# Low parts of expert weights: accumulating DMAs in place of subtractions

## The chip, the cores and the metric

The kernel runs on one core of one Trainium2 chip, as one program with an instruction stream for each engine, written out by hand with semaphores between them. The metric is the device time of one execution in microseconds, the median of several runs. Below, "span" is the time from the first to the last instruction in the one execution that was profiled.

## The reference, cut to what matters

The input is x (4 x 256 tokens of 256 values). First a gated state-space layer (a convolution, a recurrence over 256 positions with 16 states per channel, an output scaled by silu of the normalised x) is added to x. Then follows a layer of eight experts, of which each token uses two:

```
logits = x @ gate_w                       # 1024 x 8
top_logits, top_idx = top_k(logits, 2);  top_w = softmax(top_logits)
for e in range(8):
    h = silu(x @ w0[e]) * (x @ w1[e])     # w0, w1: 8 x 256 x 512
    out += cw[:, e] * (h @ wo[e])         # wo: 8 x 512 x 256
```

All is float32.

## The kernel before, in words

**Split products.** The expert products run on operands in a rounded float32 format (`fp32r`). To keep the precision each operand is split into a rounded part ("hi") and what is left ("lo"), and a product is the sum of three terms: x_hi w_hi + x_hi w_lo + x_lo w_hi (`product`, L1048). So w0 and w1, 4 MB each, need a hi and a lo copy in SBUF. Each is cut into 16 parts of 128 x 512 (expert e, half k), 32 in all, in the order of `SPLITS`: w1 of experts 0 to 5, w0 of all, w1 of experts 6 and 7. The last sit on space that other tiles occupy until the end of the scan. ScalarE rounds a part (`upper`, L529), and after that one of three engines subtracts: GpSimd 22 parts (`lower`, L405), VectorE six (`lower`, L1343), TensorE four (`low_part`, L994 and L995: the part times the identity plus the rounded part times its negative, moved out by ScalarE at L688).

**Scan.** From about 36 to 149 us the recurrence runs in 64 steps n over 128 x 512 tiles. In a step VectorE computes the drive (L1243) and the scan (L1249), ScalarE the decay as an exponential (L619) and every second step a copy of the C rows (L615), GpSimd the product of state and C (`times_C`, L414), TensorE the sum over states in PSUM (L853) and the spread of B and C rows (L832, L839). Four state buffers go round (`RING`), so VectorE's drive of step n waits for GpSimd's product of step n - 4. The tuples `SPLIT_AT` and `UPPER_AT` give the steps in which ScalarE rounds a part; GpSimd subtracts that of `SPLIT_AT` after its product of the same step. Other tuples put softplus steps, normalisations and logits of the first half of the tokens into the scan.

**Routing.** After the scan the second half is gated, normalised and routed; VectorE works out the tiles of tokens (23 `SLOTS` of 128 rows, each for one expert), TensorE makes the tables by one-hot matmuls (L1020, L1025). SyncE's queue is in order: the store of the first half (`store_x2`), WO loads of 0.5 MB each (L335) as their space comes free, two stores of normalised rows `x_rows` to DRAM (L325) and another store. GpSimd waits for both `x_rows` stores and the table, and gathers rows of a tile by an indirect DMA (L438). TensorE fills pauses with matmuls whose result nobody reads (`WARM`, `keep_busy`, L1013 and L1032), turns the tile (L1039), ScalarE rounds it (`xT_out`, L699), VectorE subtracts (`split_x`, L1472), and the first `gate` starts.

**Expert loop.** For each of the 23 tiles TensorE does gate, up (six matmuls each, L1048), the turn of the hidden tile (L1070) and down (twelve, L1084). x tiles are turned and rounded one tile ahead. The results are added to the output by an indirect accumulating DMA of 128 rows (L452).

Of the kernel before, what the change touches and what calls it, by code (L numbers as in the profile page):

```python
# [66 lines left out]
def build(nc, x, ctx_1024, g_xattn, g_ffn, in_proj_w, conv_w, conv_b, x_proj_w, dt_proj_w, dt_proj_b,  # L67
          A_log, D, gate_w, w0, w1, wo, out):
    stack = ExitStack()
    with stack:  # L70
# [12 lines left out]
        at_W0_hi = nc.sbuf_base  # L83
# [22 lines left out]
        at_W1_hi = nc.sbuf_base  # L106
# [132 lines left out]
        SPLIT = [bank[i] for i in (4, 0, 1, 7)]  # L239
# [28 lines left out]
        W_hi_ok, W_lo_pool, W_lo_dve, xT_split = map(sem, ("W_hi_ok", "W_lo_pool", "W_lo_dve", "xT_split"))  # L268
        W_lo_ps, W_lo_act, last_hc, mask_sum, count_ps = map(sem, ("W_lo_ps", "W_lo_act", "last_hc", "mask_sum", "count_ps"))
# [23 lines left out]
        def hi_part(i):  # L293
            w, e, k = SPLITS[i]
            return (W0_hi, W1_hi)[w][:, e, k, :]

        def lo_part(i):
            w, e, k = SPLITS[i]
            return (W0_lo, W1_lo)[w][:, e, k, :]
# [56 lines left out]
        def _(pool):  # L356
# [46 lines left out]
            def lower(i):  # L403
                pool.wait_ge(W_hi_ok, i + 1)
                pool.tensor_tensor(lo_part(i), whole_part(i), hi_part(i), ALU.subtract).then_inc(W_lo_pool, 1)  # L405

            def times_C(at, end):
                for n in range(at, end):
# [6 lines left out]
                    if n in SPLIT_AT:  # L415
                        lower(SPLIT_AT.index(n))
# [40 lines left out]
        def _(act):  # L457
# [128 lines left out]
            def decay(at, end):  # L586

                for n in range(at, end):
# [12 lines left out]
                    if n in SPLIT_AT:  # L601
                        if n == SPLIT_AT[0]:
                            act.wait_ge(ld["w1"], 16 * E)
                        if SPLITS[SPLIT_AT.index(n)] == (0, 0, 0):
                            act.wait_ge(ld["w0"], 16 * E)
                            act.wait_ge(delta_copied, 2)
                            act.wait_ge(one_plus, 2 * NQ)
                        upper(SPLIT_AT.index(n))
                    if n in UPPER_AT:
                        upper(EARLY + UPPER_AT.index(n))  # L610
# [147 lines left out]
        def _(pe):  # L758
# [263 lines left out]
            low_part(3)  # L1022
# [514 lines left out]
```

## Time and profile before

| | |
|---|---|
| runs, us | 300.47, 300.55, 301.75; median 300.55 |
| span of the profiled execution, us | 296.1, so its median run has 4.45 us around the span |
| busy: PE, DVE, ACT, POOL | 261.7, 226.3, 188.1, 180.1 us |
| share of the chain that ended last: PE, DVE, POOL, ACT | 57%, 15%, 6%, 4% |
| DMA: bytes and share of 16 engines, SyncE's queue / GpSimd's | 16.41 MB, 15.8% / 6.03 MB, 12.7% |
| mean granted TensorE clock | 0.980 of full speed |

PE is TensorE (PEld its weight loads), DVE VectorE, ACT ScalarE, POOL GpSimd, SP SyncE; a "q" behind a name is the engine's sequencer. The busy shares are means over three stages with different limits, so they don't say what a change in one stage is worth. A name of a tile that lies on another's space (WO for delta and zs, for instance) is that of the first tile there.

### The profile page before, as it was taken

What the parts mean: (1) busy time and instruction counts of PE and PEld (TensorE: products, weight loads), DVE (VectorE), ACT (ScalarE), POOL (GpSimd) and SP (SyncE); (2) the same over time, 40 slices, a digit from 0 to 9 for tenths busy, and PEclk for the clock granted to TensorE, in tenths of its full rate; (3) what the DMA queues carried; (4) which work ended last, traced back from release to release, by engine and by line L of the source; (5) the groups of instructions that cost most, each with busy time, mean ns of one, the idle gap of its engine ahead of it and who ended that gap; (6) DMA issues with size and microseconds to landing.
All of it is one profiled execution on the core that took longest, in us unless ns stands there. A gap on an engine that the chain in (4) does not pass through costs nothing.

```text
span 296.1 us, 4704 instructions
## 1 busy us (share of the span) xinstructions
PE 261.7 (88%) x1170; PEld 174.6 (59%) x1171; DVE 226.3 (76%) x396; ACT 188.1 (64%) x349; POOL 180.1 (61%) x162
## 2 busy tenths in 40 slices
PE   7984696899888998888889999999999999999970
PEld 6432242334345354433366658989898989898850
DVE  2939999999999998999978967656665656565630
ACT  3894587866775657778679636575757575756540
POOL 5100469898999898999880241546464656555242
PEclk9996899999999999999999999999999999999996
DMA  7699400000000001000069520333232323333322
GB/s 235 199 395 388 158 1 0 2 1 0 0 0 3 1 0 71 0 0 2 1 213 371 199 71 19 46 63 51 57 52 54 53 53 53 53 56 50 39 22 31
DMA packets 16659, 22.70 MB, mean 77 GB/s; under 512 B 2554, under 2 KB 10274, under 8 KB 16642
## 3 DMA queue, kind: packets, MB, share of 16 engines
q1 hardware_dynamic: 11456, 16.41, 15.8%
q0 software_dynamic: 4416, 6.03, 12.7%
q10 hardware_dynamic: 770, 0.06, 0.2%
q8 instruction: 7, 0.11, 0.2%
q14 instruction: 10, 0.08, 0.1%
HBM read 17.38 MB, written 5.11 MB: 76 GB/s over the span
## 4 chain that ended last, share of the span: by engine, by line
PE 57%; DVE 15%; issue 13%; POOL 6%; ACT 4%; DMA 1%; POOLq 1%; DVEq 0%; SPq 0%; ACTq 0%
PE PZ L1084 11%; PE PD L1048 11%; PE PU L1048 11%; PE PY L853 6%; DVE states L1243 6%; POOL hC L414 5%; PE PY L1070 4%; DVE states L1249 3%; DVE u L1169 2%; PE PZ L1039 2%; DMA early<-in_L_xattn_in_proj_w 1%; PE PZ L905 1%; PE PU L839 1%; PE PU L832 1%; PE PZ L894 1%
## 5 line engine op out<-in xcount | busy, mean ns | idle before, releaser
L414 POOL TENSOR_TENSOR hC<-states,WO 128x512 f32<-128x512 f32 x63 | 79.6, 1277 | 14.5 <-PE PY L853 9.3
L1249 DVE TENSOR_TENSOR_SCAN states<-PD,states 128x512 f32<-128x512 f32 x64 | 77.6, 1214 | 1.1 <-ACT PD L619 0.9
L853 PE MATMUL PY<-hC,ident 128*128 128x512 f32 x128 | 67.1, 607 | 4.1 <-POOL hC L414 3.9
L452 POOL DMA_INDIRECT out<-lg,y_at x23 | 36.9, 1605 | 49.5 <-ACT lg L727 41.8
L619 ACT ACTIVATE PD<-WO,Aneg 128x510 f32<-128x510 f32 x64 | 43.9, 689 | 19.2 <-DVE states L1249 16.5
L1243 DVE TENSOR_TENSOR states<-PU,WO 128x512 f32<-128x512 f32 x64 | 42.8, 671 | 0.5 <-POOL hC L414 0.4
L438 POOL DMA_INDIRECT hC<-x_rows,x_at x23 | 27.2, 1183 | 23.5 <-DMA x_rows<-u 13.6
L711 ACT ACTIVATE hidT_hi<-PY 128x512 fp32r<-128x512 f32 x23 | 13.8, 598 | 37.8 <-PE PY L1070 35.7
L1478 DVE TENSOR_TENSOR dA<-PU,dA 128x512 f32<-128x512 f32 x23 | 15.9, 692 | 28.5 <-PE PU L1048 28.5
L1490 DVE TENSOR_TENSOR WO_lo<-WO,WO_hi 128x512 fp32r<-128x512 f32 x46 | 29.8, 689 | 9.4 <-issue 9.3
L853 PEld LDWEIGHTS PY<-hC,ident 128*128 128x128 f32 x128 | 22.3, 189 | 15.5 <-POOL hC L414 11.1
L720 ACT ACTIVATE WO_hi<-WO 128x512 fp32r x46 | 26.5, 624 | 3.0 <-issue 0.6
L405 POOL TENSOR_TENSOR W_lo<-W,W_hi 128x512 fp32r<-128x512 f32 x22 | 28.4, 1296 | 0.0
L832 PE MATMUL PU<-BC,sel 128*128 128x512 f32 x32 | 16.9, 528 | 11.5 <-ACT WO L615 5.6
L615 ACT ACTIVATE WO<-PU 128x512 f32<-128x512 f32 x32 | 19.0, 593 | 12.3 <-PE PU L839 12.2
L832 PEld LDWEIGHTS PU<-BC,sel 128*128 128x128 f32 x32 | 6.2, 194 | 32.7 <-issue 31.8
L839 PE MATMUL PU<-BC,sel 128*128 128x512 f32 x32 | 17.7, 552 | 6.2 <-DVE states L1243 6.1
L1482 DVE TENSOR_TENSOR hidT_lo<-PY,hidT_hi 128x512 fp32r<-128x512 f32 x23 | 15.9, 692 | 5.1 <-ACT hidT_hi L711 4.9
L529 ACT ACTIVATE W_hi<-W 128x512 fp32r<-128x512 f32 x32 | 19.3, 618 | 0.0
L839 PEld LDWEIGHTS PU<-BC,sel 128*128 128x128 f32 x32 | 6.1, 191 | 21.5 <-issue 21.4
L1048 PE MATMUL PD<-W_hi,xT_hi 128*128 x46 | 16.4, 437 | 0.0
L705 ACT ACTIVATE dA<-PD 128x512 f32<-128x512 f32 x23 | 13.7, 597 | 4.1 <-PE PD L1048 4.1
(251 smaller groups left out, 501.2 us busy)
## 6 DMA issues: line engine op xcount, KB each, us to landing
W<-in_L_ffn_w SPq DMA_DIRECT2D x16, 512.0 KB, 10.6
WO<-in_L_ffn_wo SPq DMA_DIRECT2D x8, 512.0 KB, 6.9
xs<-in_x SPq DMA_DIRECT2D x2, 512.0 KB, 5.4
out<-xs SPq DMA_DIRECT2D x2, 512.0 KB, 3.4
x_rows<-u SPq DMA_DIRECT2D x2, 512.0 KB, 4.6
early<-in_ctx SPq DMA_DIRECT2D x1, 512.0 KB, 4.1
hC<-x_rows,x_at POOLq DMA_INDIRECT x23
out<-lg,y_at POOLq DMA_INDIRECT x23, 3.8
```

Of the source, the lines that this page charges most:

```text
L405: pool.tensor_tensor(lo_part(i), whole_part(i), hi_part(i), ALU.subtract).then_inc(W_lo_pool, 1)
L414: pool.tensor_tensor(hC[:, n % 2, :], states[:, n % RING, :], C_rep[:, pair % C_RING, :], ALU.mult).then_inc(hc_done, 1)
L438: pool.indirect_dma_start(out=x_tile[s % 2], out_offset=None, in_=x_rows, in_offset=bass.IndirectOffsetOnAxis(ap=x_at[:, s:s + 1], axis=0) ...
L452: pool.indirect_dma_start(out=out, out_offset=bass.IndirectOffsetOnAxis(ap=y_at[:, s:s + 1], axis=0), in_=y_tile[s % 2], in_offset=None, c ...
L619: act.activation(DEC[n % 2].rearrange("p (b l) -> p b l", b=QB)[:, :, 1:L], delta[2 * q + h].rearrange("p (b l) -> p b l", b=QB)[:, :, 1:L ...
L839: pe.matmul(BCR[(pair + 1) % 2], sel[:, DS + pair % DS:DS + pair % DS + 1].to_broadcast((P, P)), BC[:, pair // DS, :], start=True, stop=Tr ...
L853: pe.matmul(PY[:, h, :], ident[:, :], hC[:, n % 2, :], start=False, stop=(m == DS - 1)).then_inc(y_done, 1)
L1048: mm = pe.matmul(dest[i][:, :], x[i][:, k, :], w[:, bass.ds(expert, 1), k, :].rearrange("p o m -> p (o m)"), start=(n == 0), stop=(n == le ...
L1084: mm = pe.matmul(bank[7][:, i * DX:(i + 1) * DX], x[:, k, :], w[:, k, :], start=(n == 0 and k == 0), stop=(n == 2 and k == 3))
L1243: dve.tensor_tensor(states[:, n % RING, :], BCR[pair % 2], du[2 * q + h], ALU.mult).then_inc(dbu_done, 1)
L1249: dve.tensor_tensor_scan(states[:, n % RING, :], DEC[n % 2], states[:, n % RING, :], 0.0, ALU.mult, ALU.add).then_inc(scan_done, 1)
L1490: dve.tensor_tensor(WO_lo[i][:, cut, :].rearrange("p k n -> p (k n)"), WO[:, bass.ds(expert, 1), cut, :].rearrange("p o k n -> p (o k n)") ...
```

## The change

ScalarE no longer writes a rounded part beside the weight, but its negative over the weight itself. Groups of four parts (two experts, 1 MB) are then copied by SyncE inside SBUF to the place of the lo parts, and GpSimd issues a DMA that adds the weights once more from DRAM onto that copy: w - round(w). All 32 parts take this way, so the three kinds of subtraction go. Seven groups are issued from GpSimd inside the scan at `LOWER_AT`, the eighth after it; the eighth copy waits until the scan's tiles on its space are done with, ahead of the WO loads in SyncE's order. As only negated rounded weights are left, x tiles get a negated rounded copy as well (`xT_neg`, one more ScalarE instruction per tile), and the terms become x_neg w_neg + x_hi w_lo + x_neglo w_neg. All roundings lie in the scan. Matmuls that fill pauses are counted by `SPINS`.

```
-WARM = 1
-SPLIT_AT = (3, 6, 9, 12, 15, 18, 24, 26, 31, 33, 36, 39, 41, 44, 47, 49, 52, 54)
-UPPER_AT = (50, 53, 56, 57, 59, 60, 62)
+UPPER_AT = (3, 4, 6, 9, 11, 12, 15, 18, 20, 21, 23, 26, 28, 29, 31, 33, 34, 36, 38, 39, 41, 43, 46, 47, 49, 50, 52, 53, 55, 56, 58, 61)
+LOWER_AT = (15, 24, 32, 41, 50, 56, 62)
+SPINS = (4, 1, 2)
...
+        W0_neg, W1_neg = overlay("W0_neg", [P, E, 2, MH], at_W), overlay("W1_neg", [P, E, 2, MH], at_W + E * 2 * MH * 4)
+        W0_lo, W1_lo = overlay("W0_lo", [P, E, 2, MH], at_W0_lo), overlay("W1_lo", [P, E, 2, MH], at_W1_lo)
...
 # SyncE
+            def copy_neg(g):
+                w, e, _ = SPLITS[4 * g]
+                sp.wait_ge(W_neg_ok, 4 * (g + 1))
+                sp.dma_start((W0_lo, W1_lo)[w][:, e:e + 2, :, :].bitcast(F32), (W0_neg, W1_neg)[w][:, e:e + 2, :, :].bitcast(F32)).then_inc(W_copied[g], 16)
+            for g in range(3):
+                copy_neg(g)
+            sp.wait_ge(delta_copied, 2)
+            sp.wait_ge(one_plus, 2 * NQ)
+            for g in range(3, 5):
+                copy_neg(g)
             store_x2(0)
+            for g in range(5, 7):
+                copy_neg(g)
             sp.wait_ge(hc_done, NT - 1)
             sp.wait_ge(exp_done, NT)
             sp.wait_ge(dbu_done, NT)
+            sp.wait_ge(c_ps, NT // 2)
+            sp.wait_ge(b_ps, NT // 2)
+            sp.wait_ge(base_ps, NQ)
+            copy_neg(7)
             load_WO(0)
...
 # GpSimd
-            def lower(i):
-                pool.wait_ge(W_hi_ok, i + 1)
-                pool.tensor_tensor(lo_part(i), whole_part(i), hi_part(i), ALU.subtract).then_inc(W_lo_pool, 1)
+            def lower(g):
+                w, e, _ = SPLITS[4 * g]
+                pool.wait_ge(W_copied[g], 16)
+                pool.dma_start((W0_lo, W1_lo)[w][:, e:e + 2, :, :], (w0, w1)[w][e:e + 2].rearrange("e (k p) m -> p e k m", p=P),
+                               accum_op=ALU.add).then_inc(W_lo_in[w], 16)
...
-                    if n in SPLIT_AT:
-                        lower(SPLIT_AT.index(n))
+                    if n in LOWER_AT:
+                        lower(LOWER_AT.index(n))
...
-            for i in POOL_SPLITS:
-                lower(i)
+            for g in range(len(LOWER_AT), len(SPLITS) // 4):
+                lower(g)
...
 # ScalarE
-                act.activation(hi_part(i), whole_part(i), ACT.Copy).then_inc(W_hi_ok, 1)
+                act.activation(neg_part(i), whole_part(i), ACT.Copy, scale=-1.0).then_inc(W_neg_ok, 1)
...
-            act.wait_ge(b_ps, NT // 2)
-            act.wait_ge(c_ps, NT // 2)
             normed(range(QBLK))
-            for i in range(EARLY + len(UPPER_AT), EARLY + 9):
-                upper(i)
             x2_out(2)
             x2_out(3)
-            for i in range(EARLY + 9, len(SPLITS)):
-                upper(i)
             root(1)
...
-            for j in range(len(PE_SPLITS)):
-                act.wait_ge(W_lo_ps, j + 1)
-                act.activation(lo_part(PE_SPLITS[j]), SPLIT[j], ACT.Copy).then_inc(W_lo_act, 1)
...
                 act.activation(xT_hi[i].rearrange("p k t -> p (k t)"), bank[6][:, i * DX:(i + 1) * DX], ACT.Copy).then_inc(xT_ok, 1)
+                act.wait_ge(xT_ok, s + 1)
+                act.activation(xT_neg[i].rearrange("p k t -> p (k t)"), xT_hi[i].bitcast(F32).rearrange("p k t -> p (k t)"), ACT.Copy,
+                               scale=-1.0).then_inc(xT_neg_ok, 1)
...
 # TensorE
-            def low_part(j):
-                i = PE_SPLITS[j]
-                pe.wait_ge(W_hi_ok, i + 1)
-                pe.matmul(SPLIT[j], ident[:, :], whole_part(i), start=True, stop=False)
-                pe.matmul(SPLIT[j], neg_id[:, :], hi_part(i).bitcast(F32), start=False, stop=True).then_inc(W_lo_ps, 1)
+            def spin(times):
+                for _ in range(times):
+                    pe.matmul(PD[1][:, :], ident[:, :], W1_neg[:, 0, 0, :].bitcast(F32), start=True, stop=True)
...
-            for j in range(3):
-                low_part(j)
-            for _ in range(WARM):
-                pe.matmul(TABLE, ident[:, :], W1_hi[:, 0, 0, :].bitcast(F32), start=True, stop=True)
+            spin(SPINS[0])
...
-            low_part(3)
+            spin(SPINS[1])
...
-                terms = [(x, w, k) for x, w in ((xT_hi, hi), (xT_hi, lo), (xT_lo, hi)) for k in range(2)]
+                terms = [(x, w, k) for x, w in ((xT_neg, neg), (xT_hi, lo), (xT_neglo, neg)) for k in range(2)]
...
-                pe.wait_ge(xT_ok, s + 1)
+                pe.wait_ge(xT_neg_ok, s + 1)
...
-            keep_busy(1)
+            spin(SPINS[2] // 2)
             x_turn(0, 0, 16)
-            keep_busy(1)
+            spin(SPINS[2] - SPINS[2] // 2)
             pe.wait_ge(slots_ok, 1)
             first = expert_of(0)
-            pe.wait_ge(W_lo_pool, EARLY + len(POOL_SPLITS))
-            pe.wait_ge(W_lo_act, len(PE_SPLITS))
-            pe.wait_ge(W_lo_dve, 2)
+            pe.wait_ge(W_lo_in[0], 16 * E // 2)
             gate(0, 0, first)
             x_turn(1, 1, 16)
-            pe.wait_ge(W_lo_dve, len(DVE_SPLITS))
+            pe.wait_ge(W_lo_in[1], 16 * E // 2)
             up(0, 0, first)
...
 # VectorE
-            lower(DVE_SPLITS[:2])
...
-            lower(DVE_SPLITS[2:])
...
-                dve.tensor_tensor(xT_lo[i].rearrange("p k t -> p (k t)"), bank[6][:, i * DX:(i + 1) * DX],
-                                  xT_hi[i].rearrange("p k t -> p (k t)"), ALU.subtract).then_inc(xT_split, 1)
+                dve.tensor_tensor(xT_neglo[i].rearrange("p k t -> p (k t)"), xT_hi[i].rearrange("p k t -> p (k t)"),
+                                  bank[6][:, i * DX:(i + 1) * DX], ALU.subtract).then_inc(xT_split, 1)
```

## Rows read from the trace of the kernel before

**Rows 1.** The page's chain that ended last, by engine (shares of the span).
```profile
PE 57%; DVE 15%; issue 13%; POOL 6%; ACT 4%; DMA 1%; POOLq 1%; DVEq 0%; SPq 0%; ACTq 0%
```

**Rows 2.** Windows: stretch, length, busy PE, PEld, DVE, ACT, POOL, clock, DMA share, GB/s.
```profile
36.00:149.00 113.00, 98.68 (x288) 45.39 (x288) 111.45 (x140) 80.03 (x138) 102.12 (x84) 1.00 0.01 5
220.00:240.00 20.00, 20.00 (x126) 17.90 (x126) 12.47 (x21) 12.10 (x25) 11.66 (x9) 1.00 0.32 52
```

**Rows 3.** Groups by line: count, busy us, mean ns, idle us before and its releaser.
```profile
L414 POOL TENSOR_TENSOR hC<-states,WO 128x512 f32<-128x512 f32 x63 | 79.6, 1277 | 14.5 <-PE PY L853 9.3 <-DVE states L1249 4.4
L1249 DVE TENSOR_TENSOR_SCAN states<-PD,states 128x512 f32<-128x512 f32 x64 | 77.6, 1214 | 1.1 <-ACT PD L619 0.9
...
L1243 DVE TENSOR_TENSOR states<-PU,WO 128x512 f32<-128x512 f32 x64 | 42.8, 671 | 0.5 <-POOL hC L414 0.4
...
L405 POOL TENSOR_TENSOR W_lo<-W,W_hi 128x512 fp32r<-128x512 f32 x22 | 28.4, 1296 | 0.0
...
L529 ACT ACTIVATE W_hi<-W 128x512 fp32r<-128x512 f32 x32 | 19.3, 618 | 0.0
...
L1343 DVE TENSOR_TENSOR W_lo<-W,W_hi 128x512 fp32r<-128x512 f32 x6 | 3.8, 682 | 0.0
```

**Rows 4.** Timeline of the routing stage: start us, us, engine, line, tiles.
```profile
149.05 0.95 PE L894 MATMUL PZ<-gc,xT 128*128 128x8 f32 x8
...
149.29 5.40 POOL L405 TENSOR_TENSOR W_lo<-W,W_hi 128x512 fp32r<-128x512 f32 x4
...
149.36 3.82 SPq L335 DMA_DIRECT2D WO<-in_L_ffn_wo  x6
...
162.79 2.08 ACT L505 ACTIVATE u<-xs,nmr,rstd 128x256 f32<-128x256 f32 x4 [0.67 <-DVE nmr L1288]
...
164.90 0.37 SPq L325 DMA_DIRECT2D x_rows<-u  x1
...
168.32 1.38 POOL L438 DMA_INDIRECT hC<-x_rows,x_at  x1 [13.64 <-DMA x_rows<-u]
...
171.54 0.44 PE L1039 MATMUL PZ<-ident,hC 128*128 128x128 f32 x2
...
171.82 1.02 PE L1032 MATMUL PD<-W_hi,ident 128*128 128x512 f32 x2
172.02 0.38 ACT L699 ACTIVATE xT_hi<-PZ 128x256 fp32r<-128x256 f32 x1
...
173.99 0.73 PE L1048 MATMUL PD<-W_hi,xT_lo 128*128 x2
```

**Rows 5.** Windows of the DMA engines' work: two load stretches, a lull, scatter, gather.
```profile
16.00:20.00 4.00, 4.00 (x10) 1.71 (x10) 0.00 (x0) 3.97 (x8) 0.00 (x0) 1.00 1.05 399
151.00:164.00 13.00, 12.12 (x60) 8.40 (x59) 10.06 (x59) 12.26 (x24) 3.69 (x3) 1.00 1.02 349
164.00:165.00 1.00, 1.00 (x4) 0.38 (x3) 1.00 (x2) 1.00 (x4) 0.00 (x0) 1.00 0.26 84
196.00:198.00 2.00, 2.00 (x16) 1.87 (x16) 1.34 (x3) 0.61 (x2) 1.11 (x2) 1.00 0.57 66
198.00:199.00 1.00, 1.00 (x6) 0.82 (x5) 1.00 (x3) 0.85 (x3) 0.00 (x0) 1.00 0.40 131
```

**Rows 6.** GpSimd's two indirect DMA lines: duration ns min/median/max, first and last start.
```profile
L438 POOL DMA_INDIRECT hC<-x_rows,x_at x23: 940/1002/1421, 168.3 to 269.6; - x23
...
L452 POOL DMA_INDIRECT out<-lg,y_at x23: 1552/1587/2050, 184.3 to 290.3; - x23
```

**Rows 7.** Windows around TensorE's pause before the scan.
```profile
21.00:22.00 1.00, 0.00 (x0) 0.00 (x0) 1.00 (x4) 0.98 (x2) 0.00 (x0) 1.00 1.07 391
25.00:26.00 1.00, 0.00 (x0) 0.00 (x0) 0.97 (x2) 0.00 (x0) 0.00 (x0) 0.50 1.05 387
31.00:32.00 1.00, 1.00 (x4) 0.55 (x3) 0.91 (x1) 0.00 (x0) 0.98 (x1) 0.66 1.06 389
```

**Rows 8.** The chain in the expert loop: start us, us, what.
```profile
182.72 1.40 PE PD L1048 x6
```

More of the change, by code:

```diff
@@ L81, in build @@
         WO = sb("WO", [P, E, 4, DX])
-        at_W0_hi = nc.sbuf_base
+        at_W0_lo = nc.sbuf_base
         early = sb("early", [P, E * 2 * MH])
@@ L102, in build @@
         assert taken[0] <= E * 2 * MH
-        at_W1_hi = nc.sbuf_base
+        at_W1_lo = nc.sbuf_base
         free_W1 = sb("free_W1", [P, 6, 2, MH])
@@ L212, in build @@
                         for n, b in (("WO_hi", 0), ("WO_lo", 1)))
-        xT_hi, xT_lo = ([t[:, i, :, :] for i in range(2)] for t in (xT_hi_t, xT_lo_t))
-        W0_hi, W1_hi = overlay("W0_hi", [P, E, 2, MH], at_W0_hi), overlay("W1_hi", [P, E, 2, MH], at_W1_hi)
-        W0_lo, W1_lo = overlay("W0_lo", [P, E, 2, MH], at_W), overlay("W1_lo", [P, E, 2, MH], at_W + E * 2 * MH * 4)
+        xT_neg_t = overlay("xT_neg", [P, 2, 2, P], at_hC + QT * 4)
+        xT_hi, xT_neg, xT_neglo = ([t[:, i, :, :] for i in range(2)] for t in (xT_hi_t, xT_neg_t, xT_neglo_t))
+        W0_neg, W1_neg = overlay("W0_neg", [P, E, 2, MH], at_W), overlay("W1_neg", [P, E, 2, MH], at_W + E * 2 * MH * 4)
+        W0_lo, W1_lo = overlay("W0_lo", [P, E, 2, MH], at_W0_lo), overlay("W1_lo", [P, E, 2, MH], at_W1_lo)
         y_tile = [lg[:, i * DX:(i + 1) * DX] for i in range(2)]
@@ L238, in build @@
         TABLE = bank[3]
-        SPLIT = [bank[i] for i in (4, 0, 1, 7)]
         x_rows = nc.dram_tensor("x_rows", [TOK, DX], F32, kind="Internal").ap()
@@ L267, in build @@
             sem, ("route", "mask_ok", "rank_ps", "egap_ok", "slots_ok"))
-        W_hi_ok, W_lo_pool, W_lo_dve, xT_split = map(sem, ("W_hi_ok", "W_lo_pool", "W_lo_dve", "xT_split"))
-        W_lo_ps, W_lo_act, last_hc, mask_sum, count_ps = map(sem, ("W_lo_ps", "W_lo_act", "last_hc", "mask_sum", "count_ps"))
+        W_neg_ok, xT_split, xT_neg_ok = map(sem, ("W_neg_ok", "xT_split", "xT_neg_ok"))
+        W_lo_in = [sem("W0_lo_in"), sem("W1_lo_in")]
+        W_copied = [sem(f"W_copied{g}") for g in range(len(SPLITS) // 4)]
+        last_hc, mask_sum, count_ps = map(sem, ("last_hc", "mask_sum", "count_ps"))
         w_hi_ok, w_lo_ok = sem("w_hi_ok"), sem("w_lo_ok")
@@ L291, in whole_part, with neg_part @@
             return (W0, W1)[w][:, e, k, :]
-        def hi_part(i):
+        def neg_part(i):
             w, e, k = SPLITS[i]
[L295 to L299, printed above, removed]
+            return (W0_neg, W1_neg)[w][:, e, k, :]
         @block.sync
@@ L600, in decay @@
                         x2_out(X2_OUT_AT.index(n))
-                    if n in SPLIT_AT:
-                        if n == SPLIT_AT[0]:
+                    if n in UPPER_AT:
+                        i = UPPER_AT.index(n)
+                        if i == 0:
                             act.wait_ge(ld["w1"], 16 * E)
-                        if SPLITS[SPLIT_AT.index(n)] == (0, 0, 0):
+                        if SPLITS[i] == (0, 0, 0):
                             act.wait_ge(ld["w0"], 16 * E)
[L606 to L610, printed above, removed]
+                        upper(i)
                     if h == 0:
@@ L1026, in _ @@
             mm.then_inc(w_at_ps, 1)
-            def keep_busy(times):
-                pe.wait_ge(W_lo_act, len(PE_SPLITS))
-                for _ in range(times):
-                    pe.matmul(PD[1][:, :], ident[:, :], W1_hi[:, 0, 0, :].bitcast(F32), start=True, stop=True)
             def x_turn(s, i, loaded):
@@ L1040, in x_turn, with product @@
                 mm.then_inc(xT_ps, 1)
-            def product(hi, lo, dest, i, expert, done, split=None):
-                terms = [(x, w, k) for x, w in ((xT_hi, hi), (xT_hi, lo), (xT_lo, hi)) for k in range(2)]
+            def product(neg, lo, dest, i, expert, done, split=None):
+                terms = [(x, w, k) for x, w in ((xT_neg, neg), (xT_hi, lo), (xT_neglo, neg)) for k in range(2)]
                 for n, (x, w, k) in enumerate(terms):
@@ L1052, in gate @@
             def gate(s, i, expert):
-                pe.wait_ge(xT_ok, s + 1)
+                pe.wait_ge(xT_neg_ok, s + 1)
                 if not (isinstance(s, int) and s < 2):
                     pe.wait_ge(silu_ok, s - 1)
-                product(W0_hi, W0_lo, bank[0:2], i, expert, g_ps, split=s + 1)
+                product(W0_neg, W0_lo, bank[0:2], i, expert, g_ps, split=s + 1)
             def up(s, i, expert):
@@ L1060, in up @@
                     pe.wait_ge(hid_ok, s - 1)
-                product(W1_hi, W1_lo, bank[2:4], i, expert, u_ps)
+                product(W1_neg, W1_lo, bank[2:4], i, expert, u_ps)
             def hid_turn(s, i):
@@ L1338, in chosen_two @@
                                        mask[:, :, :].rearrange("p e t -> p (e t)"), 0.0, ALU.mult, ALU.add).then_inc(mask_sum, 1)
-            def lower(parts):
-                for i in parts:
-                    dve.wait_ge(W_hi_ok, i + 1)
-                    dve.tensor_tensor(lo_part(i), whole_part(i), hi_part(i), ALU.subtract).then_inc(W_lo_dve, 1)
             def rows_hot(j):
```

11 lines of the change are left out of this document (3 added, 8 removed).

## The prediction

> **What bounds the kernel now.** I read the chain that ended last first [rows 1]: TensorE holds 57% of it, VectorE 15%, waiting for nothing the profile shows 13%, GpSimd 6%. No engine bounds the whole, so I split the span into three stages and read each by its own rows.
>
> The scan (36 to 149 us) is VectorE's: 111.45 of 113.00 us busy [rows 2]. Its two instructions of a step, `drive` (L1243) and `scan` (L1249), waited 0.5 and 1.1 us in all 64 steps [rows 3]. GpSimd is close behind, 102.12 of 113.00 us, but not the limit.
>
> The expert loop (177 to 287 us) is TensorE's: 20.00 of 20.00 us busy, ScalarE 12.10 [rows 2].
>
> Between them lies routing. Its end is the first `gate` at 172.84 (where the spin of 171.82 is over), behind the first gather, which GpSimd started at 168.32 after a 13.64 us wait put down to the transfer `x_rows` [rows 4]. The second `x_rows` store left SyncE at 164.90, right after the last normalisation on ScalarE (162.79 plus 2.08) [rows 4]. From 151 to 164 the 16 DMA engines were busy all the time (share 1.02) with the 4 MB of WO and the first `x_rows` half; only at 164 to 165 did they fall to 0.26 [rows 5]. So `x_rows` started at once on a queue that had emptied about 1.1 us before it was issued, and arrived 3.4 us later. That is the place where the change will be felt.
>
> **The change, part by part.** The sum is made on the profiled span, 296.1 us; the median run shown is 300.55, so 4.45 us lie around the span and are taken as unchanged.
>
> *GpSimd subtractions.* 22 of 1.296 us go, 28.4 us [rows 3]: 18 in the scan (23.3 us), four after it (149.29 to 154.69 [rows 4]). The four lie in GpSimd's 13.64 us wait: nothing. The 18 can give VectorE back at most its idle time in the scan, 113.00 less 111.45 = 1.55 us [rows 2]; most of that was waiting for ScalarE, which gets more work, so I take -0.5 us, ends -1.55 and +1.0.
>
> *Seven more roundings on ScalarE in the scan.* 32 instead of 25, 7 x 0.618 = 4.3 us [rows 3], while ScalarE was busy 80.03 of 113.00 [rows 2]: hidden by its waits for the scan; that a rounding beside a softplus step in the first ten steps delays an `exp` is the +1.0 above. The same seven, and four evictions, leave ScalarE after the scan. The last `x_rows` rows wait for a chain on VectorE, so this moves nothing.
>
> *Seven accumulating DMAs issued by GpSimd among its products.* The trace has no direct DMA issued by GpSimd. Nearest are its indirect ones over 128 rows: gather 1002 ns, accumulating scatter 1587 ns median [rows 6]. A weight group has 512 rows of 2 KB: from below 1.0 us, from above 4 x 1.587 = 6.3 us. The next `hC` product stands behind it. A product may be late by what the ring of four states allows: `drive` n+4 waits for product n, and between stand two scans and two drives, 2 x (1.214 + 0.671) = 3.8 us, less the product's own 1.277 [rows 3]: about 2.5 us. I take 1.6 us, the row of the same operation: no stall, and less GpSimd time (7 x 1.6 = 11.2) than the 23.3 us removed. At 6.3 us each of the six inside the scan would stall VectorE by 3.8 us, 23 us in all. Each also waits for its copy; the copies have 6 to 11 steps (10 us and more) and 1 MB at the load rate takes 2.6 us, so that wait is empty.
>
> *The copies and accumulations as DMA work.* 8 MB of each. In the scan the engines are idle (5 GB/s [rows 2]), so the first seven copies and six accumulations cost nothing. The last ones are another matter. The accumulation after product 62 is issued when that product ends, about 149.3. The last copy waits for the last base logits (L894 until 150.00 [rows 4]) and stands on SyncE ahead of every WO load, which began at 149.36 [rows 4]: all of WO is 0.7 us later. The last accumulation follows the copy. So the stretch that was full with 4.5 MB gets 3 MB more, and `x_rows` has to queue behind what is on its own queue and share the engines with the other.
>
> Price: at the load rate (399 GB/s [rows 5]) 1 MB, 1.05 million bytes, is 2.63 us; that is the copy, and the lower end for an accumulation. Upper end from the loop: one scatter of 131 KB (196 to 198) keeps the engines busy 2 x 0.57 = 1.14 us, against 0.40 us for the gather of as much [rows 5]; eight times that is 9.1 us for 1 MB. The load is nearer in shape (2 KB rows, engines full), the scatter in operation. A plain transfer reads and writes, an addition reads twice and writes: 1.5 x 2.63 = 4.0 us, which I take, an estimate nearer to the load row. The engines are then through with the queue at 163.8 + 0.7 + 2.6 + 2 x 4.0 = 175.1, and `x_rows` lands 1.9 us later (1.3 us for its half MB, 0.6 to arrive, an estimate), 177.0 against 168.3: **+8.7 us**. The first gate also waits for these accumulations; they are over with the queue, before the tile. With 2.63 each it is +6.0, with 9.1 each +18.9.
>
> On this the Trainium skill speaks against the change more sharply: "Collectives: The Full Stack", Part 3, The bandwidth ceiling, says that an add in the DMA path halves the rate, because both sources have to be read through the same ring. By it an accumulation would be 5.3 us, and the total below 2.6 us higher. The loop's rows, with 1.14 against 0.40 us, show at least that factor for 1 KB rows; no run here shows it for a full queue.
>
> *Subtractions on VectorE (six, 3.8 us [rows 3]) and TensorE (four).* VectorE's stood in front of the first `split_x`, so that the third term of the first gate came only at 173.99 [rows 4]. The gate's six matmuls then need 1.40 us as in the loop [rows 8], where they took from 172.84 to 174.72: -0.5 us. TensorE's products and spins end before the table is ready; with 4 and 1 spins in place of 7 and 2 matmuls the table can be some 0.6 us earlier, which waits for `x_rows` all the same.
>
> *The negated x tile.* One more ScalarE instruction in each expert step, about as long as L699, 0.38 us [rows 4]. In the loop ScalarE has 7.9 of 20 us free [rows 2] and makes the tile a step ahead; `y_out`, `silu` and the rounding of WO queue behind it, 0.4 us later each, while TensorE still has the `up` product to do: nothing. Before the first gate TensorE runs a spin until 172.84 (the second L1032 of 0.86 us), and xT_hi ended at 172.40: 0.38 us plus a wait just fills that gap.
>
> *The clock.* TensorE went without work from 21 to 26; the granted clock was still 1.00 at 21 and 0.50 at 25, and came back only in 31 to 32 [rows 7]. The first tile is turned 3.2 us after the gather starts (171.54 [rows 4]), so at 180.3 with `x_rows` at 177; TensorE has nothing to do from its spin ahead of it (about 172) until then, and runs the first tile at 1.2 GHz: spin, gate and up need twice their 0.86 and 1.4 us, of which waits hide about a third. +2.5 us, ends 0 and +3.5.
>
> Sum: -0.5 + 8.7 - 0.5 + 2.5 = +10.2 us. Span 306.3, time **310.8**. The likeliest case's own range, with its prices at their ends, is 304.5 to 323.
>
> **The rivals.**
> *The added transfers don't reach `x_rows`.* The engines absorb copy and accumulations beside WO, the x rows come as before, and what is left is the gain: -1.55 in the scan and -0.5 in the gate. The queue had 1.1 us to spare before the store was issued; the case decides itself at about 3.5 us of added engine time before 165 (break-even with the 2 us of gain). For it: a share over 1.0 shows that packets overlap [rows 5]. Against it: 3 MB would have to cost little more than one MB did from 16 to 20 us, 2.63. Time 298.5; just at break-even 300.5.
> *GpSimd's descriptors are the bound.* An issue far over 2.5 us stalls the scan: at 4 us 6 x 1.5 = 9 us, at 6.3 us 23 us. For it: 512 rows against the 128 of 1.0 to 1.6 us. Against it: a direct transfer reads no index per row. If this adds to the forecast, 320 to 334.
> *Gains and delay cancel.* `x_rows` is late by 2 to 3 us only, for instance because the accumulation of product 62 is over before the WO loads are under way: 300 to 302.
>
> **How the numbers follow.** Forecast 0.57, descriptors 0.10, absorbed with gain 0.20, cancelled 0.13. What can be told from no change is 0.5%, 1.5 us. Faster (below 299.0) 0.20, same 0.13, slower 0.67. Range 299.2 to 319.5: it leaves out the best of the absorbed case, most of the descriptor case and the top prices of the forecast.
>
> **What would show it.** Right: DMA share near 1 without a gap from 151 to about 175; the wait of GpSimd's first gather for `x_rows` ends about 177; granted clock below 1.00 about 180; loop steps as long as before; the scan's VectorE idle under 1.5 us; direct DMAs of 1 to 2.5 us on GpSimd. Wrong: the first gather at 168 to 170, or a scan that ends clearly after 149, or gaps of VectorE after each accumulating DMA.

## The result and the profile after

The changed kernel takes 312.36 us (median of 310.90 to 312.96), against 300.51 us (299.34 to 301.75) for the kernel before beside it: ratio 1.0399, 95% interval 1.0348 to 1.0450. The forecast was 310.8 us. The profiled execution has a span of 310.6 us; its time was 312.41, so only 1.8 us lie around a span, in the runs of either kernel.

First the chain that ended last, by engine, which answers to [rows 1].

```profile
PE 50%; DVE 14%; issue 10%; SPq 7%; POOL 7%; ACT 6%; DMA 4%; POOLq 1%; DVEq 0%; ACTq 0%
```

What is new in it is SyncE's sequencer with 7% and DMA with 4% instead of 1%. The windows of the scan and of a piece of the expert loop, with the columns of [rows 2]:

```profile
36.00:149.00 113.00, 100.27 (x288) 46.35 (x289) 111.97 (x140) 84.94 (x146) 88.48 (x72) 0.98 0.52 126
220.00:240.00 20.00, 20.00 (x127) 17.90 (x126) 12.11 (x21) 12.97 (x28) 11.54 (x9) 1.00 0.33 52
```

VectorE is as full as before (111.97 of 113.00 us against 111.45), though GpSimd lost 13.6 us of work and the DMA engines are now half busy beside it (share 0.52). The loop has not changed. The groups by line, as in [rows 3]:

```profile
L429 POOL TENSOR_TENSOR hC<-states,WO 128x512 f32<-128x512 f32 x63 | 82.5, 1337 | 27.3 <-PE PY L859 20.1 <-DVE states L1242 5.1 <-ACT WO L627 0.8
L1242 DVE TENSOR_TENSOR_SCAN states<-PD,states 128x512 f32<-128x512 f32 x64 | 77.6, 1214 | 0.6 <-ACT PD L631 0.4
...
L1236 DVE TENSOR_TENSOR states<-PU,WO 128x512 f32<-128x512 f32 x64 | 42.9, 672 | 0.4 <-POOL hC L429 0.2
...
L544 ACT ACTIVATE W_neg<-W 128x512 fp32r<-128x512 f32 x32 | 19.8, 618 | 0.0
...
L419 POOL DMA_DIRECT2D W_lo<-in_L_ffn_w x8 | 10.6, 1328 | 7.8 <-DMA W_lo<-W_neg 7.6
```

GpSimd's issue of an accumulating DMA takes 1.33 us. The product right behind an issue is recorded as longer (1.77 us at 96.24, for instance), which is most of why the mean rose from 1277 to 1337 ns; but VectorE's drives and scans wait 0.4 and 0.6 us in all, no more than before, so no product is late by it. GpSimd's 7.6 us of idle time lie before the last one alone, which waits for its copy. The routing stage, to be laid beside [rows 4]:

```profile
146.93 2.33 DVE L1242 TENSOR_TENSOR_SCAN states<-PD,states 128x512 f32<-128x512 f32 x2
...
149.48 1.32 POOL L419 DMA_DIRECT2D W_lo<-in_L_ffn_w  x1
...
150.40 0.46 SPq L335 DMA_DIRECT2D W_lo<-W_neg  x1
...
150.92 16.20 SPq L329 DMA_DIRECT2D WO<-in_L_ffn_wo  x6
...
158.41 1.29 POOL L419 DMA_DIRECT2D W_lo<-in_L_ffn_w  x1 [7.60 <-DMA W_lo<-W_neg]
...
164.15 2.07 ACT L520 ACTIVATE u<-xs,nmr,rstd 128x256 f32<-128x256 f32 x4 [0.86 <-DVE nmr L1281]
...
167.16 1.86 SPq L319 DMA_DIRECT2D x_rows<-u  x1
...
172.69 1.41 SPq L319 DMA_DIRECT2D x_rows<-u  x1
...
181.56 1.11 POOL L453 DMA_INDIRECT hC<-x_rows,x_at  x1 [21.86 <-DMA x_rows<-u]
...
184.46 0.69 PE L1034 MATMUL PZ<-ident,hC 128*128 128x128 f32 x2 [9.03 <-DMA hC<-x_rows,x_at]
...
188.04 0.62 PE L1043 MATMUL PD<-W_neg,xT_neglo 128*128 x2
```

The six WO issues that took SyncE 3.82 us now take 16.20: it stands in the issue instruction, as it would behind a full queue (no row shows how full the queue is). The second half's rows are ready at 166.22 (164.15 plus 2.07) but leave at 172.69, and the first gather starts at 181.56 instead of 168.32. The windows of the DMA engines (the last three columns are clock, DMA share, GB/s), as in [rows 5]; the first lies in the scan, where only an accumulation was running:

```profile
86.00:88.00 2.00, 1.81 (x10) 0.97 (x9) 2.00 (x3) 1.82 (x4) 1.25 (x2) 1.00 1.13 205
...
151.00:160.00 9.00, 8.12 (x45) 7.08 (x43) 4.73 (x26) 6.80 (x11) 1.29 (x1) 0.83 1.00 235
160.00:167.00 7.00, 6.05 (x27) 3.63 (x25) 6.25 (x26) 3.94 (x9) 0.00 (x0) 0.97 1.09 278
176.00:181.00 5.00, 0.00 (x0) 0.00 (x0) 0.00 (x0) 0.00 (x0) 0.00 (x0) 0.50 1.07 387
181.00:182.00 1.00, 0.00 (x0) 0.00 (x0) 0.00 (x0) 0.00 (x0) 0.44 (x1) 0.50 0.17 64
```

The engines are full from 153 to 181: in every microsecond of that stretch the share is 0.99 or more (from 152 to 153 it is 0.52). They move 235 to 278 GB/s while additions are among the transfers and 387 when only plain ones are left; an addition alone moves 205, so 1 MB of it takes 1.049 / 0.205 = 5.1 us at shares over 1. A copy inside SBUF alone moves 393 (93 to 94 us). TensorE has nothing at all to do from 176 to 181, and its granted clock is 0.50, as it has been since 168.

So the difference of the two spans (14.5 us) adds up, each line from the rows shown here and in [rows 4] (the scans run from 29.65 to 149.05 us before and from 30.37 to 149.26 after). First and last scan before, first scan after:

```profile
29.65 1.22 DVE L1249 TENSOR_TENSOR_SCAN states<-PD,states 128x512 f32<-128x512 f32 x1
...
146.72 2.33 DVE L1249 TENSOR_TENSOR_SCAN states<-PD,states 128x512 f32<-128x512 f32 x2
```
```profile
30.37 1.22 DVE L1242 TENSOR_TENSOR_SCAN states<-PD,states 128x512 f32<-128x512 f32 x1
```

| stretch | before | after | difference |
|---|---|---|---|
| first scan instruction starts | 29.65 | 30.37 | +0.72 |
| scan | 119.40 | 118.89 | -0.51 |
| end of scan to first WO load | 0.31 | 1.66 | +1.35 |
| first WO load to first gather | 18.96 | 30.64 | +11.68 |
| first gather to third term of the first gate | 5.67 | 6.48 | +0.81 |
| from there to the end of the span | 122.11 | 122.56 | +0.45 |

The first line is nothing of the change: in the other runs with these DMAs the scan started at 29.62 to 30.77 us. The last line says little: in those runs that stretch was 121.8 to 124.4 us long. By the medians the change costs 11.85 us and not 14.5, because the profiled execution of the kernel before was faster than its median run; no trace shows in which line. The line that decides does not hang on it: three runs below without the added transfers have 18.85 to 19.50 us where the kernel before has 18.96.

### The profile page after: what moved, and what is told of

Its sections match the earlier page's. It is cut to its first block, busy times and chain, and to the rows that moved or that the text cites. A ratio compares the mean times of both kernels' runs of the same rounds, so it can differ in the third digit from the quotient of the medians.

```text
span 310.6 us, 4694 instructions
## 1 busy us (share of the span) xinstructions
PE 267.0 (86%) x1162; PEld 179.6 (58%) x1163; DVE 221.6 (71%) x390; ACT 193.0 (62%) x368; POOL 163.0 (52%) x148
## 4 chain that ended last, share of the span: by engine, by line
PE 50%; DVE 14%; issue 10%; SPq 7%; POOL 7%; ACT 6%; DMA 4%; POOLq 1%; DVEq 0%; ACTq 0%
PE PZ L1079 11%; PE PD L1043 10%; PE PU L1043 10%; SPq L329 6%; POOL hC L429 6%; PE PY L859 5%; DVE states L1236 5%; DVE states L1242 4%; PE PY L1065 3%; DMA x_rows<-u 3%; DVE u L1162 2%; PE PZ L1034 2%; PE PU L845 1%; PE PU L838 1%; PE PU L767 1%
## 5 line engine op out<-in xcount | busy, mean ns | idle before, releaser
L429 POOL TENSOR_TENSOR hC<-states,WO 128x512 f32<-128x512 f32 x63 | 82.5, 1337 | 27.3 <-PE PY L859 20.1
L1242 DVE TENSOR_TENSOR_SCAN states<-PD,states 128x512 f32<-128x512 f32 x64 | 77.6, 1214 | 0.6 <-ACT PD L631 0.4
L859 PE MATMUL PY<-hC,ident 128*128 128x512 f32 x128 | 67.9, 612 | 2.8 <-POOL hC L429 2.6
L453 POOL DMA_INDIRECT hC<-x_rows,x_at x23 | 26.5, 1151 | 33.1 <-DMA x_rows<-u 21.9
L1458 DVE TENSOR_TENSOR xT_neglo<-xT_hi,PZ 128x256 fp32r<-128x256 f32 x23 | 9.5, 412 | 17.6 <-ACT xT_hi L702 17.6
L544 ACT ACTIVATE W_neg<-W 128x512 fp32r<-128x512 f32 x32 | 19.8, 618 | 0.0
L1043 PE MATMUL PD<-W_neg,xT_neg 128*128 x46 | 17.1, 453 | 0.0
L1034 PE MATMUL PZ<-ident,hC 128*128 128x128 f32 x46 | 9.1, 279 | 9.0 <-DMA hC<-x_rows,x_at 9.0
```

Source lines behind the costliest of these rows:

```text
L429: pool.tensor_tensor(hC[:, n % 2, :], states[:, n % RING, :], C_rep[:, pair % C_RING, :], ALU.mult).then_inc(hc_done, 1)
L453: pool.indirect_dma_start(out=x_tile[s % 2], out_offset=None, in_=x_rows, in_offset=bass.IndirectOffsetOnAxis(ap=x_at[:, s:s + 1], axis=0) ...
L859: pe.matmul(PY[:, h, :], ident[:, :], hC[:, n % 2, :], start=False, stop=(m == DS - 1)).then_inc(y_done, 1)
L1043: mm = pe.matmul(dest[i][:, :], x[i][:, k, :], w[:, bass.ds(expert, 1), k, :].rearrange("p o m -> p (o m)"), start=(n == 0), stop=(n == le ...
L1242: dve.tensor_tensor_scan(states[:, n % RING, :], DEC[n % 2], states[:, n % RING, :], 0.0, ALU.mult, ALU.add).then_inc(scan_done, 1)
```

## The experiments

Theory: the copies and accumulations beside WO are work of full DMA engines and hold the x rows up. Rivals: it is the order of the queue; it is the clock; it is something else of the change (the negated x tile, GpSimd's issues). The measure is "WO to gather", from the first WO load to the first gather in the profiled execution: 18.96 us before, 30.64 after.

**Take one transfer or the other away.** The first run moves accumulations ahead so that the seventh is over before the WO loads begin. The second has no eighth copy and accumulation; GpSimd sets those low parts to zero instead. The third has both edits.

```
# first
-LOWER_AT = (15, 24, 32, 41, 50, 56, 62)
+LOWER_AT = (13, 22, 30, 37, 43, 51, 57)
```
```
# second: SyncE
-            copy_neg(7)
...
# second: GpSimd
-                lower(g)
...
+                pool.memset(W1_lo[:, 6:8, :, :].bitcast(F32), 0.0).then_inc(W_copied[7], 1)
...
```

> The seven accumulations inside the scan start earlier (steps 13 to 57 in place of 15 to 62), so that the one issued behind product 62 is over before the WO loads. Theory (engine time adds up: every MB that has to move before the last x_rows store delays it): an accumulation takes 5.2 us of the engines at the 200 GB/s seen inside the scan of the changed kernel, so 306 to 308 us against 312.4. Rival (only SyncE's own queue counts: the copy ahead of the WO loads and their blocked issue; GpSimd's queue runs beside it): 311 to 313.

> The eighth group's copy and accumulation are left out (its low parts are set to zero by GpSimd after the scan). Theory: 2.6 us of copy, 0.7 us of late start and 5.2 us of accumulation go: 303 to 305. Rival (SyncE's own queue alone): the copy in front was all of it, 299 to 301.

> Both: the accumulations start earlier and the eighth group is left out, so that between the scan and the first gather the DMA engines have what they had in the kernel before. Theory: the delay is gone and the two small gains stay (VectorE's idle time in the scan, the first gate without a wait): 298.5 to 300. Rival (part of the loss lies elsewhere, in the scan or in the loop with its extra ScalarE instruction): above 301.

| run | seventh beside WO | eighth | WO to gather, us | time, us | ratio to before, 95% |
|---|---|---|---|---|---|
| changed kernel | yes | yes | 30.64 | 312.36 | 1.0399 (1.0348 to 1.0450) |
| first | no | yes | 26.35 | 310.97 | 1.0336 (1.0262 to 1.0410) |
| second | yes | no | 24.44 | 305.55 | 1.0140 (1.0067 to 1.0212) |
| third | no | no | 18.85 | 303.73 | 1.0102 (1.0012 to 1.0193) |

The lines behind the first and the second run:

```profile
151.80 6.87 SPq L329 DMA_DIRECT2D WO<-in_L_ffn_wo  x6
...
178.15 1.10 POOL L453 DMA_INDIRECT hC<-x_rows,x_at  x1 [19.45 <-DMA x_rows<-u]
```
```profile
149.34 9.54 SPq L329 DMA_DIRECT2D WO<-in_L_ffn_wo  x6
...
173.78 1.11 POOL L455 DMA_INDIRECT hC<-x_rows,x_at  x1 [22.16 <-DMA x_rows<-u]
```

Without both, WO to gather is back to within 0.1 us of the kernel before. The seventh accumulation costs 5.6 us alone and 4.3 beside the eighth pair; the pair costs 7.5 alone and 6.2 beside the seventh. That is the theory's mechanism. The times, though, all missed their forecasts, by 3.0, 0.6 and 3.7 us, and the first run's lies at the edge of the rival's range, the third's inside it. In both of these WO to gather shrank as expected, but their scans ended later (below). In the third run WO also still starts 1.59 us behind the scan instead of 0.31, because SyncE's wait for the base logits, which came with the copy, stayed in. SyncE in the third run, by its timeline:

```profile
151.24 4.12 SPq L329 DMA_DIRECT2D WO<-in_L_ffn_wo  x6
...
165.76 0.37 SPq L319 DMA_DIRECT2D x_rows<-u  x1
...
170.09 1.12 POOL L455 DMA_INDIRECT hC<-x_rows,x_at  x1 [16.98 <-DMA x_rows<-u]
```

The six WO issues are back at 4.12 us, so their 16.20 us came with the transfers about them.

**The addition, or the bytes?** The last two groups are loaded plainly, with the same bytes from DRAM and the same copies.

```
-                               accum_op=ALU.add).then_inc(W_lo_in[w], 16)
+                               **({} if g >= 6 else dict(accum_op=ALU.add))).then_inc(W_lo_in[w], 16)
```

> The last two groups are loaded by the same GpSimd DMAs without the addition, so their low parts hold the weights themselves: it prices the addition. Theory with an addition at twice the engine time of a load: 2 x 2.6 us less, 306 to 308. With an addition at the price of a load: 311 to 313. With the 4.0 us of the prediction: 309 to 310.

308.32 us, ratio 1.0246 (1.0173 to 1.0320), between the forecasts for an addition at twice a load and at 4.0 us; WO to gather 26.46 us:

```profile
150.26 9.46 SPq L329 DMA_DIRECT2D WO<-in_L_ffn_wo  x6
...
176.72 1.08 POOL L453 DMA_INDIRECT hC<-x_rows,x_at  x1 [17.51 <-DMA x_rows<-u]
```

Two additions thus cost 4.2 us more than two loads, 2.1 each, over the 2.63 us of a load [rows 5]: 4.7 us for an addition. The estimate of 4.0 was too low.

**The queue's order.** ScalarE issues the two x_rows stores itself, each right behind its normalisation, so they don't stand behind WO on SyncE.

```
 # SyncE
-            store_rows(0)
...
-            store_rows(1)
...
 # ScalarE
             normed(range(QBLK))
+            store_rows(0)
...
             normed(range(QBLK, NBLK))
+            store_rows(1)
```

> The changed kernel with the two x_rows stores issued by ScalarE, whose queue is empty, in place of SyncE, right after the rows are written. Theory (engine time adds up; the order only moves the delay): x_rows lands some 8 us earlier, but the WO loads are over when they were, at about 180 us, and ScalarE waits for them before the first tile: 307 to 310. Rival (the place in SyncE's order is the cause): back to 300 to 303.

312.78 us, ratio 1.0416 (1.0367 to 1.0465): no gain, neither the rival's nor the one that the theory forecast. Its timeline:

```profile
149.86 22.49 SPq L324 DMA_DIRECT2D WO<-in_L_ffn_wo  x8
...
165.33 0.38 ACTq L511 DMA_DIRECT2D x_rows<-u  x1
...
173.65 1.11 POOL L446 DMA_INDIRECT hC<-x_rows,x_at  x1 [15.03 <-DMA x_rows<-u]
...
179.70 0.69 PE L1034 MATMUL PZ<-ident,hC 128*128 128x128 f32 x2 [4.92 <-DMA hC<-x_rows,x_at]
...
183.16 1.15 ACT L726 ACTIVATE WO_hi<-WO 128x512 fp32r x2 [15.90 <-issue]
184.22 0.36 ACT L702 ACTIVATE xT_hi<-PZ 128x256 fp32r<-128x256 f32 x1
```

The gather comes 8 us earlier, and the tile is turned at 179.70, yet ScalarE takes it only at 184.22: ahead of it in its order stand the wait for all of WO and for the stores, and a first rounding of WO, which starts at 183.16. The forecast had put the end of that wait at about 180. In the changed kernel the same rounding starts no later:

```profile
183.53 1.15 ACT L726 ACTIVATE WO_hi<-WO 128x512 fp32r x2 [15.91 <-issue]
```

So in this kernel the order only decides which of two waits ends last. The DMA engines are through at about 181 us in both, and both waits end with that total. The place of the stores alone is not the cause; what it would give in a kernel without ScalarE's wait, no run shows.

**The clock.** Two runs give TensorE more fill matmuls: SPINS (7, 12, 2), then (7, 18, 2), in place of (4, 1, 2).

> The changed kernel with 7, 12 and 2 idle matmuls, so that TensorE has work until x_rows lands. Theory (the clock costs what the prediction put on it, 2.5 us, beside the DMA delay): 309 to 310.5 against 312.4, granted clock 1.00 at 180 us. Rival (the clock is hidden behind the wait for x_rows): 312 to 313.

> The changed kernel with SPINS (7, 18, 2) in place of (4, 1, 2): eighteen fill matmuls ahead of the second table instead of the twelve of the earlier run, which left TensorE idle for the last 2.67 us before the first tile and let the granted clock fall to 0.66 there. Now TensorE is to have work until the tile lands at about 183 us. Theory (the transfers set the time of the tile; the clock costs only what the first gate and up take longer, 0.5 to 1 us): clock near 1.00 from 160 to 190, gather to third gate term 5.6 to 6.0 us instead of 6.48, 311 to 312 us. Rival (the prediction's term of 2.5 us is there): 309 to 310.5 us.

The first gave 312.54 us, ratio 1.0393 (1.0345 to 1.0441). Its clock stayed at 1.00 until 182, but TensorE ran out of work 2.67 us before the tile, and from 184 to 188, under the first gate, the clock was 0.50 after all; so the time is that of the rival, but the run does not test it. The second gave 312.32, ratio 1.0387 (1.0341 to 1.0433); windows from 170 and the first gate's third term:

```profile
170.00:180.00 10.00, 10.00 (x24) 4.37 (x23) 0.52 (x5) 0.00 (x0) 0.00 (x0) 1.00 1.07 379
180.00:190.00 10.00, 9.75 (x43) 6.25 (x42) 1.11 (x4) 2.87 (x7) 3.76 (x4) 1.00 0.15 42
```
```profile
180.49 1.11 POOL L453 DMA_INDIRECT hC<-x_rows,x_at  x1 [21.98 <-DMA x_rows<-u]
...
185.65 0.38 PE L1034 MATMUL PZ<-ident,hC 128*128 128x128 f32 x2
...
187.15 0.73 PE L1043 MATMUL PD<-W_neg,xT_neg 128*128 x2 [0.25 <-ACT xT_neg L704]
...
188.17 0.62 PE L1043 MATMUL PD<-W_neg,xT_neglo 128*128 x2
```

At full clock the tile's turn to the third term takes 2.52 us (185.65 to 188.17), in the changed kernel 3.58 (184.46 to 188.04), before 2.45 (171.54 to 173.99). So the clock costs 1.1 us here, and at most 1.4: in five other profiles with a clock of 0.50 there the stretch took 3.77 to 3.90 us. The run did not gain them, as its delayed table matmuls put the turn off by 2.3 us (5.16 us behind the gather's start instead of 2.90). Gather to third term took 7.68 us instead of the 5.6 to 6.0 forecast, and the 311 to 312 us were missed by that. The price of the clock is thus read from rows; no run got it back in its time, and none shows the 2.5 us that the prediction had.

**What was left in the third run.** It had 1% over the kernel before and a clock of 0.80 and 0.69 from 160 to 180. First SPINS became (7, 2, 2). Then the first four accumulations went back to their steps, and the fifth from 43 to 46 (with SPINS (6, 2, 2)):

```
-LOWER_AT = (13, 22, 30, 37, 43, 51, 57)
+LOWER_AT = (15, 24, 32, 41, 46, 51, 57)
```

> The kernel of e3 (accumulations early, eighth group left out) with 7, 2 and 2 idle matmuls of TensorE in place of 4, 1 and 2, as many as the kernel before ran there. In e3 TensorE ran out of work at 163.7 us, its granted clock fell from 1.00 to 0.50 at 166 and came back at 176, and TensorE turned the first tile 1.7 us after its gather could have let it. Theory (what is left of the loss in e3 is this clock): 299.5 to 301.5, 2 to 3 us below e3. Rival (the rest of the loss is in the scan or the loop): as e3.

> Like the run without either transfer (no copy and no accumulation of the eighth group, whose low parts are left at zero; six, two and two fill matmuls), but only the accumulations of the fifth, sixth and seventh group are issued earlier (after products 46, 51 and 57), the first four as in the changed kernel. Theory that what was left over there (WO loads from 151.2 to 152.5 us instead of 149.4) comes from the first four accumulations being issued too early in the scan: WO loads from about 149.5, first gather at about 168.5, 299.5 to 301.5 us, the same as the kernel before. Rival, that any accumulation which is moved ahead costs the scan as much: 302 to 304 us.

With the matmuls 302.86 us, ratio 1.0067 (1.0033 to 1.0102). The interval overlaps that of the third run, so no gain is shown though the clock was now 0.94 and 1.00 from 160 to 180, and the forecast was missed; the rival, that the rest of the loss lies in the scan or the loop, fits. With the other tuple 299.91, ratio 0.9966 (0.9939 to 0.9993), as forecast. The intervals don't touch: the first five accumulations, two to four steps earlier, cost about 1% there. In the traces the scan took 120.17 us with the early tuple (30.77 to 150.94) and 118.58 with the other (29.71 to 148.29). This holds throughout: the four profiles with the early tuple have scans of 119.87 to 120.17 us, the nine others after the change 118.53 to 118.89. That is 1.0 to 1.6 us of the 3; the rest is not located. Why the scan is longer is not settled: VectorE's waits put down to GpSimd's products are 0.9 us in the one and 0.2 in the other, half of it at most.

The same tuple in the changed kernel, whole:

> The changed kernel whole, with the accumulations of the fifth, sixth and seventh group after products 46, 51 and 57 instead of 50, 56 and 62; the eighth copy and accumulation stay. Theory (one accumulation of about 5 us of full DMA engines taken out from beside WO, and the scan not touched): first gather about 5 us earlier than in the changed kernel, 306 to 308.5 us. Rival (moving accumulations ahead costs the scan as much as in the earlier variant): 309.5 to 311.5 us.

308.26 us, ratio 1.0252 (1.0215 to 1.0290), as forecast; WO to gather 26.30 us. One accumulation taken out from beside WO gives 4.3 us, and 4.1 us of time.

**The eighth group on an engine.** Two whole versions keep all 1 MB transfers out of the routing stage: one adds the eighth group on GpSimd (weight plus ScalarE's negated part), the other on TensorE, as the kernel before did with four parts. They differ in the tuple as well: the first has the early one (13, 22, 30, 37, 43, 51, 57), the second the other (15, 24, 32, 41, 46, 51, 57).

```
 # GpSimd, first version
+                pool.wait_ge(W_turned, j + 1)
+                pool.tensor_tensor(lo_part(i), whole_part(i), lo_part(i), ALU.add).then_inc(W_lo_pool, 1)
...
 # TensorE, second version
+                pe.wait_ge(W_turned, j + 1)
+                pe.matmul(SPLIT[j], ident[:, :], whole_part(i), start=True, stop=False)
+                pe.matmul(SPLIT[j], ident[:, :], lo_part(i).bitcast(F32), start=False, stop=True).then_inc(W_lo_ps, 1)
...
```

> A whole kernel: accumulations early, the eighth group by ScalarE (negated rounded copy beside the weight, later once more over it) and four GpSimd additions in its idle time, no copy and no accumulation after the scan, 6, 2 and 2 idle matmuls. Theory: DMA traffic between scan and first gather as in the kernel before, clock kept, 0.5 us less at the first gate and up to 1.5 us less in the scan: 299 to 301, 0 to 2 us below the kernel before. Rival (the seven roundings and accumulations in the scan cost what they free): 0 to 2 us above it.

> The whole computation: seven groups by accumulating DMAs as in the kernel just described, the eighth group as in the kernel before on TensorE (ScalarE writes the negated rounded part, TensorE adds weight and negated part in PSUM, ScalarE moves the sum out and then negates the weight in place), so that neither a copy nor an accumulation stands beside WO and nothing of GpSimd stands beside VectorE's routing. Theory (the loss is all DMA work in the routing stage, and the additions on GpSimd stretched VectorE in the earlier variant): first gather at 168 to 170 us, 299 to 301.5 us, no slower than the kernel before. Rival (the negated copy of x, the missing work on GpSimd or the later rounding cost something that the other runs hid): 303 to 306 us.

The first was a miss: 308.23 us (302.74 to 310.28), ratio 1.0269 (1.0212 to 1.0326). Its profiled execution is its fastest. With the early tuple its scan takes 119.97 us, and it shows a second cause, on VectorE's chain that leads to the second x_rows store:

```profile
159.00 1.27 POOL L448 TENSOR_TENSOR W_lo<-W,W_lo 128x512 fp32r<-128x512 f32 x1 [8.71 <-ACT W_lo L691]
159.08 1.34 DVE L1347 TENSOR_TENSOR_SCAN upto<-carry,mask 128x64 f32<-128x64 f32 x1
...
161.09 3.72 POOL L448 TENSOR_TENSOR W_lo<-W,W_lo 128x512 fp32r<-128x512 f32 x3 [0.82 <-ACT W_lo L691]
162.44 1.18 DVE L1373 TENSOR_TENSOR first_slot<-tile_end,tiles 128x8 f32<-128x8 f32 x1
```

In the changed kernel, with GpSimd waiting, the same two take 0.29 and 0.14 us:

```profile
157.92 0.29 DVE L1330 TENSOR_TENSOR_SCAN upto<-carry,mask 128x64 f32<-128x64 f32 x1
...
161.79 0.14 DVE L1356 TENSOR_TENSOR first_slot<-tile_end,tiles 128x8 f32<-128x8 f32 x1
```

A VectorE instruction that reads two operands from SBUF stood until GpSimd's addition beside it was over. The Trainium skill ("SBUF — State Buffer", Who interferes with whom) states this: such an instruction contends with a GpSimd one that reads SBUF, and the later waits for the whole of the earlier. The rows agree (1.34 us against 0.29). What made its other executions 4.2 to 7.5 us slower still was not seen.

The second version met its forecast in time, 300.80 us (299.72 to 301.79), ratio 1.0015 (0.9982 to 1.0047), the same as the kernel before; its first gather comes at 170.84, 0.8 us later than forecast.

```profile
148.61 3.98 SPq L336 DMA_DIRECT2D WO<-in_L_ffn_wo  x6
...
167.24 0.37 SPq L326 DMA_DIRECT2D x_rows<-u  x1
...
170.84 1.12 POOL L454 DMA_INDIRECT hC<-x_rows,x_at  x1 [22.25 <-DMA x_rows<-u]
```

It does seven eighths of the change, negated x tile and all, and neither gains nor loses: what cost 12 us was the last eighth and the late seventh. Its WO starts 0.42 us behind the scan, without the wait for the base logits. No version here beats both kernels: the one at 0.9966 leaves a group's low parts out.

## Why the prediction came out right, point by point

- **Bounds of the stages**: right. VectorE bounds the scan, TensorE the loop, and the second x_rows store the routing.
- **GpSimd subtractions, -0.5 us**: the scan is 0.51 us shorter in the one pair of profiles, and 0.5 to 0.9 us shorter than that one scan of before in all nine profiles whose first four accumulations stand at their steps; with the early tuple it is longer. No more than that is shown; 13.6 us less work on GpSimd brought nothing else.
- **Roundings on ScalarE, issues on GpSimd**: right. 1.33 us for an issue where 1.6 was taken; no product stalled. The rival of the descriptors falls.
- **Delay of the x rows, +8.7 us**: the mechanism was right, the size too small: +13.0 in WO's start and WO to gather (1.35 and 11.68). The term that was mis-sized is the accumulation: 4.0 us taken, 4.3 to 5.6 by the runs with and without it, 4.7 by the loads in its place, 5.1 by its rate alone. At 4.7 to 5.1 each, two of them are 1.4 to 2.2 us of the 4.3. WO started 1.35 us later instead of 0.7, because the copy waits for the base logits and is issued first; the wait alone does most of it (1.09 to 1.64 us behind the scan in the runs without the copy, 0.42 in the two without the wait). The rest is slack: 2.6 us (0.7 + 2.6 + 8.0 less 8.7) were taken as free at the end of the queue; with 2.6 for the copy and 2 x 5.1 the 11.68 leave about 1.1.
- **The rule of the Trainium skill** ("Collectives: The Full Stack", Part 3, The bandwidth ceiling, on the reduce step of a collective), that an addition halves the rate because both sources are read through one ring: 205 against 399 GB/s agree with it, and its 5.3 us were closer than the 4.0 that the prediction preferred. That it holds for the reason given there, no run shows.
- **The first gate, -0.5 us**: not there. At full clock the turn to the third term takes 2.52 us against 2.45: the negated tile, 0.42 us on ScalarE ahead of the gate, took what VectorE's subtractions had cost. The prediction had put the negated tile at nothing; at full clock the gate's first matmul waits for it (0.25 us at 187.15).
- **The clock, +2.5 us**: it fell, as said (to 0.50 from 168 to 186), but costs 1.1 us in the first gate by the rows, and in the table at most the 0.45 of the last line behind it.
- **Around the span, 4.45 us**: wrong. 1.8 us lie around any span; the profiled execution of before was thus itself 2.6 us faster than the median run (296.1 + 1.8 against 300.55), and the prediction carried that as a constant.
- **Sum**: on the profiles +10.2 us forecast, +14.5 measured. The delay was 4.3 us short; the gate and the clock, +2.0 forecast, came to 1.26 with the rest of the loop; the later start of the scan is chance. In the time the 4.45 us gave 2.65 of the missing 4.3 back (310.8 = 296.1 + 10.2 + 4.45, against 312.4 = 296.1 + 14.5 + 1.8). So the cause was right, but that the total came as near as 1.6 us is luck: a delay put too small and a constant put too large cancelled in part.
- **The rivals**: "absorbed" and "cancelled" fall with the ratio. What decided against them stands in the table of runs: each MB beside WO has nearly its full price, for the queue had about 1 us to spare.

## What to carry to other kernels

In this kernel, work moved from an engine to the DMA queues was free only where the DMA engines were idle, so place every transfer by the DMA share of its stretch: seven eighths of this change cost nothing in the scan, and an eighth and the one before it cost 12 us behind it. Count an accumulating transfer as about two (205 against 399 GB/s here). Then ask who is waiting for the end of the queue; here two engines were, so giving one transfer another queue moved the wait and not the end.

## What was not expected of the hardware

- SyncE's issue of a 0.5 MB load is no constant: six take 3.8 to 4.3 us without the added transfers and 16.2 us with a copy and two additions about; in the run without x_rows stores between them, eight take 22.5 us. Stores behind them leave late although their data is ready.
- An accumulating DMA costs GpSimd 1.3 us of issue for 1 MB, and VectorE's scans and drives beside it keep their 1214 and 672 ns (before 1214 and 671); but issued two to four steps earlier, five of them made the scan 1.0 to 1.6 us longer. An ordinary addition on GpSimd stretched a small VectorE instruction from 0.14 to 1.18 us.
